# Moving the first layer normalisation of a graph network into the build of its adjacency blocks

## The reference

```
h = relu(layernorm(x, eps=1e-5)); x = x + sage(relu(sage(h)))     # two SAGE layers (mean of neighbours)
h = relu(layernorm(x));           x = x + segment_sum(w * (h@W)[src], dst) + b
h = relu(layernorm(x));           x = x + message net: scatter, MLP with skips, two inner layernorms (eps 1e-6)
h = relu(layernorm(x));           x = x + h@W_self + mean over neighbours of top32(h@W_neigh)
layernorm(x) = (x - mean) / sqrt(var + eps)
```

## Time and profile before

| | us |
|---|---|
| median of 3 runs | 1964.8 (1963.81 to 1965.75) |
| the profiled execution, its own time | 1964.03 |
| its span | 1962.2 |
| build, first product of PE to its last | about 46 to 575 |
| handover (no aggregation on PE) | 574.7 to 621.1 |
| sage1, sage2 | 621 to about 1040 |
| gcn | about 1050 to 1400 |
| inter | about 1415 to 1800 |
| maxk | about 1800 to 1962 |

### The profile page before, as it was taken

How to read it: one execution, slowest core, us unless ns; L and a number is a source line. 1 busy time by engine, 2 the same in 40 slices (tenths; PEclk the granted TensorE clock), 3 DMA queues, 4 the chain that set the end, 5 groups by cost and what they waited for, 6 DMA issues and landing times.

```text
span 1962.2 us, 47621 instructions
## 1 busy us (share of the span) xinstructions
PE 1721.2 (88%) x11659; PEld 1285.1 (65%) x11660; DVE 1141.7 (58%) x3359; ACT 736.6 (38%) x2169; POOL 364.9 (19%) x980
## 2 busy tenths in 40 slices
PE   2998999998973999999997999999888888884996
PEld 1555555555542777768886888888665566652886
DVE  5888888888786222223335666666367677774111
ACT  0988898888871111111111222222122222221000
POOL 1555555555543000000000000000011111110000
PEclk8999999999996999999998999999899999996998
DMA  2544554554463666633344665655211111110444
GB/s 64 163 134 123 154 152 122 161 144 123 133 201 98 173 174 175 178 105 132 118 135 124 180 170 156 181 164 159 71 53 60 60 53 52 52 52 17 150 150 149
DMA packets 302398, 246.01 MB, mean 125 GB/s; under 512 B 144042, under 2 KB 286182, under 8 KB 302310
## 3 DMA queue, kind: packets, MB, share of 16 engines
q1 hardware_dynamic: 302310, 245.19, 41.8%
HBM read 138.17 MB, written 99.31 MB: 121 GB/s over the span
## 4 chain that ended last, share of the span: by engine, by line
issue 61%; PE 26%; DVE 5%; POOL 2%; ACT 2%; DVEq 1%; ACTq 1%; SPq 0%; POOLq 0%; DMA 0%
PE ps L1249 17%; PE ps L1299 7%; POOL work L578 2%; ACT front L599 1%; DVE front L837 1%; DVE front L835 1%; ACT work L593 1%; PE ps L1234 0%; DVE work L958 0%; PE ps L1280 0%; ACTq L329 0%; DVE arena L969 0%; ACTq L338 0%; DVE arena L766 0%; ACTq L599 0%
## 5 line engine op out<-in xcount | busy, mean ns | idle before, releaser
L1299 PE MATMUL ps<-arena 128*128 128x256 f16 (+1 forms) x5000 | 597.9, 273 | 48.4 <-POOL arena L568 38.9
L1299 PEld LDWEIGHTS ps<-arena 128*128 128x128 f16 x5000 | 487.5, 98 | 146.4 <-issue 78.3
L1249 PE MATMUL ps<-front 128*128 128x400 bf16 x2580 | 480.4, 340 | 23.6 <-ACT front L599 20.5
L599 ACT ACTIVATE front<-front 128x128 bf16<-128x128 bf16 x1290 | 407.4, 389 | 55.9 <-issue 32.9
L1249 PEld LDWEIGHTS ps<-front 128*128 128x128 bf16 x2580 | 240.3, 99 | 195.8 <-ACT front L599 30.4
L1293 PE MATMUL ps<-arena 128*128 128x256 f32 x1250 | 280.3, 381 | 0.0
L556 POOL TENSOR_SCALAR front<-front,w_col 128x128 bf16<-128x128 bf16 x645 | 243.9, 384 | 164.5 <-DVE front L835 159.1
L578 POOL TENSOR_TENSOR work<-work 128x256 f32<-128x256 f32 x75 | 55.5, 740 | 1106.1 <-ACT work L702 1106.1
L1293 PEld LDWEIGHTS ps<-arena 128*128 128x128 f32 x1250 | 237.0, 191 | 31.5
L837 DVE TENSOR_SCALAR front<-iota,off_g,front 128x400 bf16<-128x400 f16 x645 | 253.9, 394 | 0.0
L835 DVE TENSOR_SCALAR front<-iota,front 128x128 bf16<-128x128 f16 x645 | 162.5, 252 | 89.0 <-PE ps L1249 68.5
(11 more groups left out here) (179 smaller groups left out, 1460.9 us busy)
## 6 DMA issues: line engine op xcount, KB each, us to landing
arena<-turned_blocks SPq DMA_DIRECT2D x75, 800.0 KB, 4.3
wgt_blocks<-arena SPq DMA_DIRECT2D x25, 1600.0 KB, 8.5
arena<-wgt_blocks SPq DMA_DIRECT2D x25, 1600.0 KB, 8.2
cnt_blocks<-work SPq DMA_DIRECT2D x25, 800.0 KB, 4.2
turned_blocks<-arena SPq DMA_DIRECT2D x25, 800.0 KB, 3.5
e_raw<-edge_features_padded SPq DMA_DIRECT2D x25, 576.0 KB, 7.8
edge_features_padded<-in_edge_attr SPq DMA_DIRECT2D x24, 512.0 KB, 9.5
out<-arena SPq DMA_DIRECT2D x24, 128.0 KB
```

The lines of the kernel that those rows point to most:

```text
L599: m = act.activation(part_of(u, O_SW + a * P, P), part_of(u, O_S, P), ACT.Copy, scale=one(col[:, c, :], t))
L1249: return pe.matmul(out_, left, right, start=False, stop=True, skip_group_check=True)
L1299: m = pe.matmul(agg[par][:, 0:wide], BLK16[par][:, b * P:(b + 1) * P], ZH[zin(i)][:, b * ZW + part * D:b * ZW + part * D + wide], start=(b ...
```

## The change

- The first normalisation leaves the handover. Within the walk of tile c, between groups (`after(t)`), DVE does bn_stats of tile c-1 after group 2, bn_aggr after group 3 and the reciprocal after group 5; ACT the square root after group 4; POOL subtracts the mean after group 5 and multiplies after group 6 (as tensor_tensor with a broadcast operand). One tile later DVE does the relu after group 0, ACT the float16 copy after group 2, POOL the low part after group 4. The last tile's steps, and the tail of the one before, stand behind the walks. H_SCALE goes into the scale and the bias of the square root.
- To allow for that, the walks of tiles 1 and 2 are written out ahead of the loop (ACT, DVE; tile 1 alone on POOL); the loop makes 11 passes of two tiles instead of 12.
- The scale of the first layer (`convolution_scale`, `spread_largest`) goes into the first step of sage1: DVE does it ahead of `mean_and_own(0)`, PE after the first aggregation.
- SP loads the transposed blocks 0 and 1 between the stores of tile 23 and tile 24.
- Everywhere `variance` goes: eps is the bias of ACT's square root, which bn_aggr now releases (`spread`). In `outer_and_top` two of its slots and two drains go.

```diff
+            for n in range(2):
+                sp.wait_ge(s_store_c[n], 16)
+                sp.dma_start_transpose(BLK16[n].rearrange("p (b d) -> p b d", d=P),
+                                       cnt_dram[n * P:(n + 1) * P, :]).then_inc(s_blk[n], 16)
             store(NT - 1, 0)
...
+            def first_norm(n, step):
+                if step == 0:
+                    wait(pool, s_scale0, n + 1)
+                    pool.sem_inc(s_made, 1)
+                row, op, by = ((node(X, n), ALU.subtract, mv[:, 0:1]), (node(R_, n), ALU.mult, rs))[step]
+                pool.drain()
+                m = pool.tensor_tensor(node(R_, n), row, by.broadcast_to([P, D]), op)
...
+                def after(t):
+                    if not isinstance(c, int) and t == 4:
+                        second(c - 2)
+                    if not (isinstance(c, int) and c == 0) and t in (5, 6):
+                        first_norm(c - 1, t - 5)
...
+            def first_deviation(n):
+                wait(act, s_var0, n + 1)
+                act.activation(sd, mv[:, 1:2], ACT.Sqrt, bias=eps_first, scale=1.0 / H_SCALE ** 2).then_inc(s_std0, 1)
+            def first_high(n):
+                wait(act, s_zD, n + 1 + CR)
+                act.activation(span(ZH[0], n * ZW, D), node(R_, n), ACT.Copy).then_inc(s_z0, 1)
...
+                def after(t):
+                    late(t)
+                    if not (isinstance(c, int) and c == 0) and t == 4:
+                        first_deviation(c - 1)
+                    if not (isinstance(c, int) and c < 2) and t == 2:
+                        first_high(c - 2)
...
+            def first_stats(n):
+                dve.bn_stats(bn, node(X, n))
+                dve.drain()
+            def first_variance(n):
+                dve.bn_aggr(mv, bn).then_inc(s_var0, 1)
+            def first_scale(n):
+                wait(dve, s_std0, n + 1)
+                dve.reciprocal(rs, sd).then_inc(s_scale0, 1)
+            def first_relu(n):
+                wait(dve, s_norm0, n + 1)
+                dve.tensor_scalar(node(R_, n), node(R_, n), 0.0, None, ALU.max).then_inc(s_zD, 1)
...
-            def variance(eps):
-                return dve.tensor_scalar(ve, mv[:, 1:2], eps, None, ALU.add).then_inc(s_var, 1)
+            def spread():
+                dve.bn_aggr(mv, bn).then_inc(s_var, 1)
```

More of the change, by code:

```diff
@@ L350, in after @@
                     take(c, par, t - 1)
-                elif not isinstance(c, int):
+                elif not (isinstance(c, int) and c == 0):
                     take(c - 1, 1 - par, PER - 1)
@@ L557, in weigh_last @@
                                        ALU.mult, ALU.mult).then_inc(s_hotP, 1)
[L558 to L572, removed]
+                def after(t):
[3 more added lines that the diff above has]
+                        first_norm(c - 1, t - 5)
+                walk(pool, mybir.EngineType.Pool, c, weigh_last, after=after)
+            weigh_and_norm(0)
+            weigh_and_norm(1)
+            with pool.Fori(2, NT) as c:
+                weigh_and_norm(c)
+            second(NT - 2)
+            for k in range(2):
+                first_norm(NT - 1, k)
+            second(NT - 1)
             def mlp_sums(n):
@@ L645, in row_phase @@
                 z(NT - 1, g0 + NT - 1, (g0 + NT - 1) % 2)
[L648 to L655, removed]
             def copy_conv(n):
@@ L838, in hot, with after @@
                                       ALU.add, ALU.is_equal).then_inc(s_hotQ, 1)
+                late = one_tile_late(take, c, par)
+                def after(t):
+                    late(t)
+                    if not (isinstance(c, int) and c < 2) and t == 0:
+                        first_relu(c - 2)
+                    if not (isinstance(c, int) and c == 0):
+                        if t == 2:
+                            first_stats(c - 1)
+                        if t == 3:
+                            first_variance(c - 1)
+                        if t == 5:
+                            first_scale(c - 1)
                 wait(dve, s_store_w[par], half * 16)
-                walk(dve, mybir.EngineType.DVE, c, hot, after=one_tile_late(take, c, par))
+                walk(dve, mybir.EngineType.DVE, c, hot, after=after)
             hot_and_take(0, 0, 0)
-            with dve.Fori(0, NPAIR) as j:
+            for j in range(NT // SB):
+                dve.wait_ge(s_x[j], 16 * (1 + (j == NT // SB - 1)))
+            hot_and_take(1, 0, 1)
+            hot_and_take(2, 1, 0)
+            with dve.Fori(1, NPAIR) as j:
                 hot_and_take(j * 2 + 1, j, 1)
@@ L954, in _ @@
                     dve.wait_ge(s[par], 16 * ((NT + 1 - par) // 2))
[L955 to L969, removed]
-                                      one(rs_all, n), ALU.subtract, ALU.mult)
-                dve.drain()
-                for c in range(SB):
-                    n = j * SB + c
-                    dve.tensor_scalar(node(R_, n), node(R_, n), 0.0, H_SCALE, ALU.max, ALU.mult).then_inc(s_zD, 1)
             dve.sem_inc(s_row, NT)
-            dve.drain()
             def mean_and_own(n, g, par):
```

129 lines of the change are left out of this document (74 added, 55 removed).

## The result

The changed kernel takes 1991.8 us (median of 4 runs, 1989.1 to 1994.94) against 1965.3 (1963.81 to 1966.56) for the kernel before in the same set: ratio 1.0136, 95% interval 1.0117 to 1.0154. I had forecast 1930 with a range of 1910 to 1972: wrong in sign, and outside the range. The profiled execution took 1994.94, its span is 1993.2.

A forecast was written before the change was run, and what follows sets the result against it. PE and ACT both bound the build; the handover is a chain with PE nearly idle. From 1964.0: handover -31, build +32, table load +1, loop end -30, later norms -6 and -1, giving 1929, against the median 1930; range 1910 to 1972.

The forecast's parts named there:

- Rival B: Build pays more than the handover gives: 1992 us with 36 us more and the stall kept, 1974 with half; chance 0.15.
- The build's insertion: Build: work added after groups stalls PE 1.35 us a tile over 24 tiles, +32 us; bounds 0 and +91.
- wait for the reciprocal: Build, after group 5: POOL waits for DVE's reciprocal, then takes 0.74, first piece 0.6 late; stall 0.50 us a tile.
- slack of 0.5 us: Build: POOL's first piece ends at 456.12 and PE needs it at 456.6, leaving POOL 0.5 us a group.
- B's mechanism: Build, groups 4, 5 and 6: POOL and DVE hold up each other and the ring of three.
- upper price for that rule, 36 us: Build: if POOL blocks DVE's one-hot writes for whole instructions, three POOL steps a tile cost up to 36 us more.
- The loop end: Build: ACT's stall behind its loop branch costs about 33 us; its going gives -30, or -3 if one body stalls.
- both bodies being free: Build: ACT's and DVE's loop bodies, placed anew by the change, both avoid the loop-end stall; chance 0.45.
- The handover: Between build and sage1: only the last tile's normalisation is left, first transpose at 598.8; -31 us, bounds -26 to -35.
- wait that I had put at 586 for the store: Handover: DVE still waits for the weight block's last store, put at 586, before the 9.8 us of scale work.
- The later norms: Inter: no addition and drain, reciprocal about 0.4 earlier, -6 us (0 to -11); sage2 and gcn ends -1.

The follow-up runs named there:

- e9: The changed kernel with 80 empty semaphore increments heading ACT's program and 175 spread over DVE's preparation, moving both loop bodies: 1965.8 us, ratio 1.0001 to the kernel before.
- e1: The kernel before with 150 empty semaphore increments in front of ACT's program, so only ACT's code moves: 1931.5 us, ratio 0.9831.
- e4: The changed kernel without the drain behind bn_stats; a semaphore orders bn_aggr a group later instead: 1981.6 us, ratio 1.008 to the kernel before.
- e3: The changed kernel with POOL's three steps of the first normalisation on one column instead of 256: 1981.2 us, ratio 1.0089 to the kernel before.
- e5: The kernel before with three unused POOL additions of 128 x 256 float32 a tile, behind groups 4, 5 and 6: 1991.0 us, ratio 1.0138.
- e2: The changed kernel with 80 empty increments heading ACT's program and 135 heading DVE's: 1998.1 us, ratio 1.0168 to the kernel before.
- e8: The kernel before with ACT's program shifted by 150 increments, transposed blocks 0 and 1 loaded before the last store, convolution's scale behind the first aggregation: 1933.3 us, ratio 0.9844.
- e11: As e8, with statistics ahead of the last weight store's wait and PE's scale steps behind the first aggregation's first piece: 1923.3 us, ratio 0.9793 to the kernel before.
- e6: The kernel before with the changed kernel's later norms, epsilon as the square root's bias instead of an addition on DVE: 1965.8 us, ratio 1.0005.
- e7: As e6, but the later norms' square root has no bias and epsilon is left out: 1949.9 us, ratio 0.9926 to the kernel before.

## Why the prediction was wrong

Two steps failed, the price of the inserted work and the placing of the loops, and a third, smaller term was mis-sized. Against the profiled execution the sum of 1929 lacks 66 us: some 31 at the first, 33 at the second, 6 at the third, less 4 of the handover. Rival B, to which I gave 0.15, said that the build pays more than the handover gives, at a kept stall, and that is what happened. That its 1992 is the measured time is in good part luck: its 36 us were the price of DVE's and POOL's holding each other up, and that is not what PE waited for.

**The build's insertion, the main failure: +32 forecast, +63 measured.** At stalled loops the build grew by 66.2 us, at free ones by 63.3 (557.8 in e9 against 494.5 in e1). Per step, us a tile:

| after group | forecast | measured | what the runs show of it |
|---|---|---|---|
| 2, statistics and drain | 0.40 | 0.82 | 0.5 is the drain (e4); 0.3 before ACT's product, by bn_stats or ACT's copy |
| 3, bn_aggr | 0.10 | 0.07 | |
| 4, low part on POOL, root | 0.15 | 0.50 | 0.3 at POOL's product, goes with the width (e3); 0.2 at ACT's, stays |
| 5, reciprocal, subtraction | 0.50 | 0.68 | all at POOL's product; 0.2 goes with the width, behind which the wait for the reciprocal appears |
| 6, multiplication | 0.15 | 0.51 | nearly all at POOL's product; 0.4 goes with the width |
| 0, relu | 0.05 | 0.12 | |

At 2 I had counted DVE's busy time against ACT's and left out that a drain exposes the register work of the next group's first instruction. At 4 and 6 the step that failed is the slack. I had set each of POOL's steps alone against a slack of 0.5 us, as if it were there anew in each group, and had left out the 0.3 us that POOL stands before such a step. At 5 I had priced a wait for the reciprocal, which POOL does in 3 tiles of 24. Three steps in three successive groups use the slack up in the first; from then on POOL needs 2.7 to 2.9 us a group, and PE takes its pace.

What I called B's mechanism, one-hots held up by POOL's additions, is real too. I had put it aside by one row, the L837 of 0.45 beside a POOL scaling in the earlier trace rows, and carried that over to additions on 256 float32 columns, though the L1131 row was the nearer one: its mean of 638 ns hides two cases, 11 that begin 0.05 us before an addition of POOL and take 0.92 us, and 14 others that take 0.41. e5 confirms it, 378 ns becomes 777. But in the changed kernel, by the products that start late, it is not what costs: POOL's piece comes last. The Trainium skill ("SBUF — State Buffer", on the shared port pair) says that the two engines then block each other for a whole instruction; the trace agrees for one-hots beside POOL's additions (777 ns), and not beside its bf16 scalings (378, at most 0.5 us). The prediction's upper price for that rule, 36 us, is near the 31 us by which the term was short, but that is chance: of the 63 us POOL's width accounts for 21 by e3 and the drain for 13 by e4, neither of them by held one-hots as far as the products show.

**The loop end: -30 forecast, +3 or so measured.** The forecast put 0.45 on both bodies being free. Neither was. The two gaps fall together in time, so that the second adds little (e2 closes one of them and wins 3 us), and together they cost 36.7 us (e9 against the changed kernel). The +3 are the 66.2 at stalled loops less the 63.3 at free ones. The price of a stall was right (33 us forecast, 33.8 by e1), the place was a guess. By my count of the queues' records, with one unrecorded instruction added for each inner loop, the bodies begin at these instructions of their programs (good to a few: e9's 175 increments appear in the count as 172):

```
ACT   177 (360 long) stalls   327 (360) free   521 (370) stalls   602 (370) free
DVE   228 (360) free          579 (374) stalls 714 (374) stalls   751 (374) free
```

The Trainium skill ("Runtime: NRT & Kernel Launch", "Instruction fetch mechanics") has two blocks of 256 instructions held at a time. ACT's four fit that at a small shift of the count; DVE's four fit it at no shift, unless a body needs some more room than its own length. That rule, used as I used it, does not tell a free place from another, and which rule does stays open.

**The handover: -31 forecast, -35.0 measured, right.** PE's first aggregation begins 6.5 us after the last close (7 forecast), the transpose 20.3 after it (24 forecast). The wait that I had put at 586 for the store is real: DVE stands 5.44 us in it, in shadow of the aggregation. What the sum lacked is seen in e8 and e11: before the change DVE's scale work, which I booked as the start of the chain, only covered that same store, and taking the scale away alone gives nothing.

**The later norms: -7 forecast, -1.0 measured.** The removed addition is real, but the epsilon moved into the square root costs 92 ns (294 against 202), which I had put at nothing without a row. e6 gives the sum of both, nothing; e7 shows what the missing one would have been worth, twice the term, because the clock in inter then falls once instead of six times.

With the two stages' prices at their measured size and the loops free, the change is +63 - 35 + 2 (a later start in e9) + 4 (the rest; inter alone takes 5 more, with eight stretches at the lower clock instead of five) = +34 us on e1. At free loops it loses 34 us, at stalled ones 26.

## What to carry to other kernels

An engine's slack in a ring is spent once: add up the engine's whole program for a group, the gaps between its instructions included, and compare it with the period, instead of setting each added step against the slack. A dummy instruction of the same shape shows the size of the cost first (e5 is a few lines and gave 25 us of build, against the 66 of the change), and which product starts late shows whose it is. Before costing a change at a loop, see whether the loop's own end stalls: 150 empty instructions moved this kernel by 33 us, more than the change itself, and the change, an edit ahead of DVE's loop, made that loop stall unasked. Where an engine works during a wait for a DMA, taking that work away gives nothing until the wait goes too.

## What the runs showed of the hardware

- The pause at a loop's end is 2.3 to 3.1 us where it occurs and 0.2 to 0.3 where not, on ACT and on DVE, for bodies of 360 to 374 instructions; only the position differs between e1 and the kernel before.
- A pause that PE has to sit out costs more than itself: eleven pauses of 2.4 us cost 33.8 us. With them the build's granted clock is at 0.50 for seven stretches, 27.2 us together; without them (e1) only in its first 5.5 us, where it is low in the kernel before too (4.5 us).
- A DVE one-hot of 400 columns beside a POOL addition on 128 x 256 float32 takes 777 ns instead of 378 when it starts at most 0.11 us behind it; beside a scaling of 128 x 128 bf16 it takes 378, at most 0.5 us.
- ACT's square root on 128 x 1 takes 294 ns with a bias from SBUF and 202 without; one over the root with a bias also takes 293.
- In inter 92 ns less a square root ended five of the six stretches at the lower clock. Whoever prices that chain by its length alone gets, by the estimate at e7, 5 of the 14 us.
